# A first sweep over half segments and a reordered front, with a new order in the combine stage and in the last stage

## The reference, cut to what matters

```python
x = ln(x + attn0(x)); x = ln(x + moe(x)); x = ln(x + attn1(x)); x = ln(x + ffn1(x))
# attn0: u = x Wi^T, sp = x Ws^T;  state = tanh(state A^T + u B^T) + sp;  out = (state C^T) Wo^T + bo
# moe: softmax gate over 8 experts, the two best; relu(x w1) w2 each, weighted by the gate
# attn1: 16 heads of 64, layer norm on q and k, causal softmax, then Wu
# ffn1: sigmoid(xr Wr) * (relu(xk Wk)^2 Wv); xr and xk mix a token with the one before it
```

## Time and profile before

| | us |
|---|---|
| median of 3 runs | 2423.36 (2419.03 to 2669.99) |
| the profiled execution | 2420.41 |
| its span on the slowest core, core 7 | 2418.8 |
| spans of the eight cores | 2395.6 to 2418.8 |
| busy on core 7: PE, ACT, DVE, POOL | 1990.1, 809.2, 698.0, 440.0 |

### The profile page before, as it was taken

One profiled execution on the slowest core, in us unless ns is written; L12 is line 12 of the kernel. 1 busy time (PEld: TensorE's weight loads), 2 busy tenths in 40 slices (PEclk: granted clock), 3 DMA queues, 4 the chain that ended last, 5 costly groups with the idle time before them and its releaser, 6 DMA issues.

```text
span 2418.8 us, 25623 instructions; the slowest of 8 cores (2395.6 to 2418.8 us)
## 1 busy us (share of the span) xinstructions
PE 1990.1 (82%) x10564; PEld 999.2 (41%) x10545; DVE 698.0 (29%) x1357; ACT 809.2 (33%) x1159; POOL 440.0 (18%) x484
## 2 busy tenths in 40 slices
PE   5662999999999999999999447786887886486576
PEld 2111656656474655647465223332332332232233
DVE  5543001010101001010100256543444442544453
ACT  2222312203030211203021025576877874422322
POOL 1124202011110201011010122101322321122232
PEclk9675999999999999999999778998998999798888
DMA  9784999989799997979792476400013214300100
GB/s 283 230 209 158 172 171 195 169 172 169 147 173 171 161 174 155 174 153 177 145 174 64 152 211 182 124 0 2 18 27 57 59 27 81 103 35 35 52 35 35
DMA packets 135351, 304.30 MB, mean 126 GB/s; under 512 B 55840, under 2 KB 61729, under 8 KB 133156
## 3 DMA queue, kind: packets, MB, share of 16 engines
q0 software_dynamic: 49296, 169.90, 39.9%
q1 hardware_dynamic: 85908, 132.46, 20.2%
HBM read 367.06 MB, written 69.34 MB: 180 GB/s over the span
## 4 chain that ended last, share of the span: by engine, by line
PE 61%; ACT 12%; DVE 10%; issue 10%; POOL 4%; DMA 3%; SPq 1%; POOLq 0%; ACTq 0%; DVEq 0%
PE ps L1434 60%; ACT PT L1434 6%; ACT rsd L1434 3%; DVE PT L1434 3%; POOL x3f L1434 2%; DVE lstf L1434 1%; ACT sq L1434 1%; DVE xk L1434 1%; DVE rf L1434 1%; DMA sumC<-stg 1%; DVE xt L1434 1%; DVE lsmf L1434 1%; DMA xTf<-xT 1%; POOL lsmf L1434 1%; ACT x3b L1434 1%
## 5 line engine op out<-in xcount | busy, mean ns | idle before, releaser
L1434 PE MATMUL ps<-xgT,W 128*128 128x320 bf16 x4096 | 559.5, 300 | 23.3 <-DMA xgT<-xgs 22.9
L1434 PE MATMUL ps<-W,hT 128*128 128x512 bf16 x2560 | 553.8, 379 | 0.0
L1434 ACT ACTIVATE hT<-ps,cf 128x640 bf16<-128x640 f32 x256 | 203.2, 794 | 834.1 <-PE ps L1434 834.1
L1434 PEld LDWEIGHTS ps<-xgT,W 128*128 128x128 bf16 x4096 | 401.3, 98 | 181.3 <-issue 23.0
L1434 PEld LDWEIGHTS ps<-W,hT 128*128 128x128 bf16 x2560 | 250.5, 98 | 300.8
L1434 DVE TENSOR_TENSOR yst<-ps,b2r 128x1024 f32<-128x1024 f32 x40 | 49.0, 1224 | 914.8 <-PE ps L1434 914.8
L1434 ACT ACTIVATE PT<-ps 128x1024 bf16<-128x1024 f32 (+7 forms) x384 | 271.8, 791 | 78.7 <-PE ps L1434 75.1
L1434 POOL DMA_DIRECT2D W<-w x256 | 135.6, 538 | 856.6 <-PE ps L1434 805.4
L1434 PE MATMUL ps<-PT,Vg 128*128 128x512 bf16 (+3 forms) x640 | 195.1, 366 | 55.2 <-DVE PT L1434 54.6
L1434 PE MATMUL ps<-qz,KT 128*128 128x512 bf16 (+3 forms) x640 | 189.5, 364 | 17.7 <-POOL qz L1434 12.1
L1434 DVE TENSOR_TENSOR PT<-PT,cb 128x128 bf16<-128x128 bf16 x256 | 111.5, 454 | 174.4 <-ACT PT L1434 171.8
(11 more groups left out here) (216 smaller groups left out, 1604.9 us busy)
## 6 DMA issues: line engine op xcount, KB each, us to landing
W<-w POOLq DMA_DIRECT2D x256, 512.0 KB, 39.3
ybs<-yst SPq DMA_DIRECT2D x40, 512.0 KB, 5.4
xgs<-zero SPq DMA_DIRECT2D x20, 512.0 KB, 16.6
xTf<-xT SPq DMA_DIRECT2D x8, 1024.0 KB, 18.0
xt<-x SPq DMA_DIRECT2D x16, 512.0 KB, 9.6
x1s<-xt SPq DMA_DIRECT2D x16, 512.0 KB, 5.0
x1c<-x1s SPq DMA_DIRECT2D x32, 256.0 KB
x2s<-x1c SPq DMA_DIRECT2D x16, 512.0 KB, 3.0
```

The costliest lines, as they stand in the source:

```text
L1434: ins = getattr(eng, method)(*args, **kw)
```

## The change

Front: the first sweep runs over positions 32 to 63 alone (`WARM = 32`), from zero; so 96 steps in place of 128. Chunks of x are loaded and cast in the order 2, 3, 0, 1; the second sweep's c matmuls, and those of chunk 1's sp, hang on the steps of the second sweep. States of tiles 0 to 14 are formed on DVE at steps of their own (`state(i)`). After the sweep, PE does the output matmuls of two tiles (`z_mm`) before DVE's `pair` adds and normalises them; `gate_y`, `route` and `rank` (split off from `route`, one group later) and `gate_x` of the next group are put between pairs. ACT takes the second statistics of tiles 9 and 13 alone (before: 7, 9, 11, 13, 15). Up to two tiles are scattered behind each tile.

Combine: x1 of tiles 0 and 1 go to a place of their own (`x1e`) that is free one matmul phase earlier; x1 of tiles 0 to 2 are issued ahead of WqS, and WkS only after the first two units. `v_tile` runs one tile late, between the two units; the transposes are between them too; `qk_tail` hangs after the sixth matmul. The memset of `Vg` goes behind tile 15's combine.

Last stage: head 15 is normalised in two halves, with a reciprocal of 64x1024 on DVE and one DMA each; Wu tiles 0 to 7 wait for the first half only. `mix(0, 0)` is cut in four, behind tiles 4 to 7; `wu_tile(8..15)` come one `rv_tile` later and `x3_transp` ahead of them; the final layer norm goes into `finish(i)`, behind the Wu tile and the mix; the scale's last product moves from DVE to POOL.

```diff
-    for n in range(128):
-        sweep, s_ = divmod(n, 64)
+    for i in range(NTILE - 1):
+        at(n2 + 4 + 4 * i, lambda i=i: state(i))
+    for n in range(n2 + SEG):          # n2 = SEG - WARM
+        sweep = int(n >= n2)
+        s_ = n - n2 if sweep else WARM + n
...
+        z_mm(i)
+        z_mm(i + 1)
+        gate_y(nt)
+        if nt > 0:
+            ranked(nt - 1)
+        if nt < 3:
+            route(nt)
+            gate_x(nt + 1)
...
+        pair(i)
+    tile_n(NTILE - 1, True)
+    route(3)
+    ranked(3)
+    some(NTILE)
```

```diff
-            if k == 4 and pend:
+            if k == 6 and pend:
...
-            for g in (2 * j, 2 * j + 1):
-                qk_unit(WqS, t_wq, g, nt, QT[g], qlw, qlb)
-            if i < NTILE:
-                back(i)
+            v_last = i - 1
+            qk_unit(WqS, t_wq, 2 * j, nt, QT[2 * j], qlw, qlb)
+            if v_last < NTILE:
+                v_tile(v_last)
+            if i < NTILE:
+                turn(i)
+            qk_unit(WqS, t_wq, 2 * j + 1, nt, QT[2 * j + 1], qlw, qlb)
```

```diff
+    def half_norm(half):
+        cs = slice(half * 1024, (half + 1) * 1024)
+        t = DV("reciprocal", stg[1][0:64, cs], stg[1][0:64, cs], w=(at1["ev", 30 + half],))
+        t = DMA("sync", f"dh{half}", recB[1][64:128, cs], stg[1][0:64, cs], w=(t, at1["ao", 13]))
+        at1["hn", half] = DV("tensor_tensor", aoT[7][64:128, cs], stg[1][64:128, cs], recB[1][64:128, cs], ALU.mult,
+                             w=(t,))
...
         for q in range(4):
-            rv_tile(4 * nt + q)
+            i = 4 * nt + q
+            rv_tile(i)
+            if 2 <= i <= 9:
+                x3_transp(i + 6)
+            if 1 <= i <= 8:
+                wu_tile(i + 7, wu_mm(i + 7, range(8)))
             if nt + 1 < 4:
-                mix(nt + 1, 0, (2 * q, 2 * q + 1))
+                mix(nt + 1, 0, (2 * q, 2 * q + 1) if nt == 0 else ((), (0, 1, 2), (3, 4, 5), (6, 7))[q])
+            finish(i)
```

More of the change, by code:

```diff
@@ L273, in build @@
     t_xf = {}
-    for nt in range(4):
+    for nt in (2, 3, 0, 1):
         for h in range(2):
@@ L439, in spread @@
             at(t0 + (t1 - t0) * j // len(items), f)
[L441 to L456, removed]
+    cbank = (0, 1, 5, 7)
+    n2 = SEG - WARM
+    spread([sp_mm(3, k) for k in range(8)], 0, 6)
+    at(6, sp_ev(3))
+    at(7, lambda: cast_x(0))
+    spread([c_mm(st, 3, k, 3, "c1") for k in range(10)], 7, 15)
+    at(8, cast_o)
+    spread([sp_mm(0, k) for k in range(8)], 16, 21)
+    at(21, sp_ev(0))
+    at(22, lambda: cast_x(1))
+    at(22, woc)
+    spread([c_mm(st, 0, k, cbank[0], "c2") for k in range(11)], 23, n2)
+    spread([sp_mm(1, k) for k in range(8)], n2, n2 + 6)
+    at(n2 + 6, sp_ev(1))
+    spread([c_mm(st, 1, k, cbank[1], "c2") for k in range(10)], n2 + 7, n2 + 15)
+    at(n2 + 16, woc_t)
+    at(n2 + 24, gate_sums)
+    at(n2 + 60, bound)
+    spread([c_mm(st, 2, k, cbank[2], "c2") for k in range(10)], n2 + 20, n2 + 30)
+    spread([c_mm(st, 3, k, cbank[3], "c2", "sg") for k in range(10)], n2 + 34, n2 + 46)
     ahead = 6
-    for n in range(47, 128):
-        if late and not (n >= 70 and (n - 70) % 10 < 4):
-            at(n, late.pop(0))
     def post(S, nx):
@@ L686, in build, with z_mm @@
             f()
+    assert not sched
+    state(NTILE - 1)
+    adds = {}
+    def z_mm(i):
+        mms, adds[i] = tile_z(i, True, i % 4 == 1)
+        for f in mms:
+            f()
+    z_mm(6)
+    z_mm(7)
     t = DV("tensor_tensor", dif[:, 0:NSEG - 1], tanh[:, T - NSEG:T - 1], e1[:, 1:NSEG], ALU.subtract, w=(st["h", 15],))
@@ L694, in build, with some, pair, ranked @@
     routed = []
-    for i in range(ahead, NTILE + 1):
-        if i < NTILE:
[L697 to L701, removed]
-            nt = (8, 10, 12, NTILE).index(i)
-            gate_y(nt)
-            route(nt)
-            routed += range(4 * nt, 4 * nt + 4)
-            if nt < 2:
-                for c in range(4 * nt, 4 * nt + 4):
-                    load_w2(0, c, w=(st["xgm", nt],))
-        for _ in range(2 if len(routed) > 6 else 1):
+    def some(n):
+        for _ in range(n):
             if routed:
                 scatter(routed.pop(0))
-    for i in routed:
-        scatter(i)
+    def pair(i):
+        for j in (i, i + 1):
+            adds[j]()
+            tile_n(j - 1, j > ahead + 1)
+            some(2)
+    def ranked(nt):
+        rank(nt)
+        routed.extend(range(4 * nt, 4 * nt + 4))
+    gate_x(0)
+    pair(6)
+    for nt in range(4):
+        i = 8 + 2 * nt
+        z_mm(i)
[6 more added lines that the diff above has]
+            gate_x(nt + 1)
+        if nt < 2:
+            for c in range(4 * nt, 4 * nt + 4):
+                load_w2(0, c, w=(st["xgm", nt],))
+        pair(i)
[3 more added lines that the diff above has]
+    some(NTILE)
     ends()
@@ L735, in build @@
             S["h", i] = t
-        load_x, tile_z, tile_all, tile_n, gate_x, gate_y, route, scatter, ends = post(S, 2)
+        load_x, state, tile_z, tile_all, tile_n, gate_x, gate_y, route, rank, scatter, ends = post(S, 2)
         for i in range(2):
@@ L1009, in front, with turn @@
             fetch(i + 2)
-    def back(i):
+    def turn(i):
         transp(i, x2b[i % 2], x2T[i // 4][:, :, (i % 4) * 128:(i % 4 + 1) * 128], "x2b")
-        v_tile(i)
+    for i in range(3):
+        fetch_x1(i)
+    t_wq = DMA("sync", "wq", WqS, wc_d[0].rearrange("(c p) m -> p c m", p=128), w=(t_m1,) + t_wc)
+    t_cb2 = DMA("sync", "cb2", cb2, cb_d[:, 384:640], w=(t_m2,))
     for i in range(2):
```

120 lines of the change are left out of this document (70 added, 50 removed).

## The result

The changed kernel takes 2334.75 us (median of 4 runs; before, beside it, 2424.87). The ratio is 0.9607, with a 95% interval of 0.9549 to 0.9665: 95 us less, 81 to 109. This ratio and all that follow leave out the runs in which the cores of one die took longer at a lower granted clock, and where too few runs were left for an interval (e1, e6, e10), the fastest run stands in its place. The profiled execution takes 2326.70 us; its slowest core, 7 again, spans 2324.8.

The account below looks back on a forecast made before the run. PE bounds the experts; elsewhere step chains, waits and loads do. Gains of 47 (front), 6 (combine), 18 (last head) and 26 (K part to end) sum to 97 us: 2323, or 2326 on the median; own spread 2300 to 2350.

Parts of the forecast that it names:

- The front: Sweep and tail ahead of the experts: gain of 47 us, experts starting at 199.6 against 246.7; bounds 35 to 59.
- the spacing of 5.61: Front, SP's queue: the next x load follows the first by 5.61 us, taken as little more than a store's landing.
- The walk of DVE's list: Front's tail: five pairs 47 us, four routes 20, ranks 6 and 2.5 more, putting the last rank at 178.
- Rival (1): Front's tail stays serial or x loads rule: front gains 22, half the last stage's gain comes, 2364 us; chance 0.14.
- The combine stage: Start gains 18 us, loop loses 12.5, end gains 3.4 less 5 for the memset: 6 in all, range -8 to 25.
- The last head and the Wu tiles: Last head to the K part: gain of 18 us, from 7.6 and 11.4 less 1.2; bounds 8 and 24.
- the 8 x 0.8 of the forecast: Eight tiles up to the K part: DVE no longer waits for POOL's power in the scale, 0.8 us each.
- the 5 us that I gave the cut of the mix: Eight tiles up to the K part: cutting the 9 us mix in four was given 5 of 11.4 us.
- From the first K part: K part to end: gain of 26 us, from 20, 14.7, minus 7.5 and minus 1.5 by group; bounds 5 and 45.
- Rival (3): Last head's reciprocal and port cost more, last stage loses its gain in third and fourth group: 2361 us; chance 0.07.
- Rival (4): Sweep: 32 steps from zero are too few, so a plain scan of 2048 steps adds 942 us: 3265; chance 0.02.
- Rival (2): The combine loop isn't closed and the last stage's last two groups lose nothing: 2292 us; chance 0.12.

Follow-up runs that it names:

- e1: The kernel before with the front's part of the change alone; fastest run 2391.9 us.
- e6: The changed kernel with ten of the twenty zero stores issued at the sweep's last step, behind the x1 stores and x loads listed by then; fastest run 2330.9 us.
- e10: The changed kernel with head 15 normalised as in the kernel before (three DRAM trips, reciprocal of 128x16, one product); fastest run 2344.5 us.
- e5: The changed kernel with the first eight W2 loads (4 MB) issued behind the last scatter; ratio to before 0.9664.
- e4: The changed kernel with the first eight W2 loads issued one behind each of tiles 8 to 15, not in two bursts; ratio to before 0.9653.
- e9: The changed kernel with 32 idle steps between the two sweeps, so the chain has 128 steps again; ratio to before 0.9617.
- e7: The changed kernel with the combine loop in its old order, the new start kept; ratio to before 0.9611.
- e12: The changed kernel with the combine loop in its old order and the Vg memset in sixteen pieces over tiles 4 to 15; 2327.48 us, ratio to before 0.9594.

## Why the prediction was right in its sum, and wrong in two terms

**The front: forecast 47, measured 28.8 (core 7: 30.8), below even the bound of 35.** Right: the state's wait gone, the sweep's end (82.7 for 79 to 82), the first x load (96.20 for 97.5) and with it the first add (101.22 for 102.5), eight scatters at the end. The stretch from the last scatter to the experts came out 1.5 us longer than I had left it (14.1 for 12.6 from issue to matmul). Wrong: "zero fill and stores move the same bytes after the change, so I leave the load where it is". It was right for the first load, and I kept the spacing of 5.61 for all the following, though the kernel before already had two of some 16 us behind its W2 loads. The walk of DVE's list gave the waits for x no term; they are 4.76, 2.35 and 3.59 of the 15 us by which the last run of scatters comes late. The same bytes had to move in less time: DMA at 0.88 and 242 GB/s against 0.64 and 186 from 102 to the last scatter before. Of the moved steps I had not counted the W2 loads that stand with `route`; they now leave at 111 and 123, where they left at 130 and 153. Rival (1) named this growth of the spacing, but priced the front at 22. That it is the volume is shown by e5 (4 MB less, the last scatter 12 us earlier, near my 188), that the order of the same bytes doesn't help by e4 and e6, and that the sweep's length hardly matters by e9 with e6.

**The combine stage: forecast 6, measured 7.6 through the attention, and about right piece by piece.** Start 20.2 for 18. Loop minus 9.4 for minus 12.5: the period was right, 12.89 for 12.9, but of the ten periods before two were already 12.95 us long, not the 11.65 that I had taken for all, and after the first was still 11.65. End minus 2.8 for minus 1.6. The memset costs 7, shown by e7 against before and e12 against e7, where I had put 5: it meets the normalisation of tile 15, not a small operation. Which of the three edits made the start shorter, WkS behind, x1 first or the memset away, no run tells apart.

The rule of the Trainium skill that I weighed ("SBUF — State Buffer", section "SBUF: two separate sides": the port pair's lock is held for a whole instruction) agrees with this trace and decided the memset's price: the normalisation takes 7.39 beside a memset of 6.92, and 0.81 without it.

**The last head and the Wu tiles: forecast 18, measured 16.7.** On core 7 the first add is 9.5 us closer to the last evacuation (27.65 to 18.17; forecast 7.6), the tiles take 46.5 in place of 53.1, 6.6 less (forecast 11.4). e10 gives the halves alone 10. The trace tells which part of the 11.4 fell short. DVE's waits for POOL in the scale, eight of 0.66 to 0.69 us before, are gone, which is about the 8 x 0.8 of the forecast. Its other waits among these tiles add up to 12.3 us, where they were 10.8: after the cut DVE waits 4.39 for the first transposed tile instead of 3.49, and for x2 where it didn't wait before. DVE, after:

```profile
2026.21 1.23 DVE L1514 TENSOR_TENSOR x3f<-ps,x2t 128x1024 f32<-128x1024 f32 x1 [2.80 <-DMA x2t<-x2s]
```

So the 5 us that I gave the cut of the mix, for which no row stood, did not come. No run has the one edit without the other.

The Trainium skill ("VectorE: DVE Perf Modes", section "First, the fixed hardware budget") gives a repeat count of 8; my estimate of 8.5 us, which took that count for the cost of one element, is not borne out. The reciprocal of 64x1024 takes 6.54, near the 6.7 scaled from the row of before (0.10 us over 16 elements is 6.3 ns, not my 6.5, and gives 6.6), and the measurement decides.

**From the first K part: forecast 26, measured 40.6.** I had cut the stage at the end of each stall. On core 7, with each cut at the matmul behind the last wait ahead of or in a K part, the four groups give 25.9, 19.2, minus 3.3 and minus 0.1 us, forecast 20, 14.7, minus 7.5 and minus 1.5. So all four directions were right, and every size was too low, by 1 to 6 us each. In the first group I had put four tiles at 12.2; in fact no Wu tile stands behind the group's first, three behind the others, and PE goes through them almost without waiting, at 6.9 to 11.2, 39.9 us in place of 48.8; the K part itself took 15.11 for 16.18. The second group's tiles, at 10.8 to 12.5, are near my 12.2. For the third I had written that there is no Wu tile to fill; the eighth now stands there, behind `rv_tile(8)`, and takes some 4 us from the first group into this one. I had also read the 16.58 of the earlier trace rows as the time from one R product to the next; it is the longest of three, but the sum didn't use it.

So the sum was met by luck of two errors, minus 18 and plus 15. Rival (3) is out, as neither the last head nor the last stage lost. Rival (4) didn't come: no scan of 2048 steps runs in any of these traces. Rival (2) is out, as the loop's period of 12.89 shows. Open is why the attention takes 338 to 353 us on different cores of one kernel (e12; 338 to 343 in the changed kernel), from its first matmul to its last evacuation; that spread limits what these times can tell from each other.

## What to carry to other kernels

When a stage is tightened, add up the bytes that must move within it, and divide them by its new length: a stage bound by latency before may be bound by transfers after, and then neither order nor shorter chains help, only bytes that go elsewhere at no cost. Before work is moved on an engine, write down what it did in a neighbour's shadow; two evacuations of 1 us that were free cost 1.2 us a tile inside the chain. A wait that the old kernel's slowness covered is no wait in its trace: look at the queue's spacing over the whole stage, not at its first two entries. A long POOL instruction on SBUF belongs beside DVE work that waits anyway, or in pieces.

## What the runs showed of the hardware

A transposed read of 6.06 us took 29.53 with 4.2 MB of loads from another queue issued ahead of it (e5): 23.5 us more, which is 179 GB/s if those bytes are all that it waited for. The Trainium skill ("DMA: Bandwidth & Descriptors", section "Queues, rings and completion order") says that each DMA engine goes round its queues packet by packet; no run here separates that from plain order. Stores of 512 KB landed in some 5 us in a quiet stretch and in 15 to 16 behind a 2 MB burst. A DVE normalisation of 128x1024 lasted 7.39 us beside POOL's memset of 6.92, at most 1.45 beside pieces of 0.5 (e12), and 0.81 otherwise. The reciprocal of 1024 elements a partition took 6.54 us, 6.4 ns an element.
